# Projecting the third and fourth batch earlier in layer 0's attention

## Chip, cores and metric

One NeuronCore of a Trainium2 chip runs the whole kernel in one launch. The metric is the device time of that launch in microseconds (us), lower is better.

## What is computed

Two transformer layers on x of shape 4 x 512 x 256 (batch, sequence, width), each with attention and a mixture of experts, both modulated. Only layer 0's attention (16 heads of 16) is touched by the change:

```python
h = _layernorm(x) * (1 + ca) + sa
q, k, v = (h @ w.T + b for w, b in (wq, bq), (wk, bk), (wv, bv))   # 4 x 16 heads x 512 x 16
q, k = _apply_rope(q, k, S)
attn = softmax(einsum('bhqd,bhkd->bhqk', q, k) / sqrt(16))
ctx = einsum('bhqk,bhkd->bhqd', attn, v)
x = x + ga * (ctx @ wo.T + bo)
```

The rest (layer 0's experts, layer 1's attention, layer 1's experts) follows in the same program and is the same in both kernels.

## The kernel before

Layer 0's attention works on 16 groups G of four heads, four groups to a batch b. A **step** s is one round of a loop written out in Python; in it each engine gets, in program order, what its function (`tensor`, `vector`, `scalar`, `gpsimd`, `sync`) lists for s. Engines run their own instructions in that order and wait for others by semaphores, so the table of steps sets the order on every engine.

Group G owns steps 8G to 8G+7 for its scores. The line L778 appears twice on TensorE in each step (two matmuls, the scores of two heads), so the n-th pair of L778 in the trace starts step n. Batch b's scores are steps 32b to 32b+31: the third batch (b = 2) starts at step 64, the fourth (b = 3) at 96. The steps of a group after its scores are fixed offsets from 8G:

- every step: VectorE takes the maximum of two score rows (L790, `vector_max`). The scores of step s+2 use the same PSUM banks and wait for it.
- 8G+8: GpSimd splits the maxima (L802 and L804, `gpsimd_ncol`). 8G+9: TensorE turns them (L815, `tensor_nT`). 8G+10: ScalarE copies the row (L824), and GpSimd issues four small DMAs (L834, `gpsimd_nmax`) that put them beside the queries.
- 8G+13 to 8G+20: TensorE computes the turned scores (L854), which wait for those DMAs at 8G+13; ScalarE takes the exponential (L869, twice a step); TensorE multiplies by the values (L883) in every second step from 8G+16. The first of these waits for VectorE's transpose of the group before.
- 8G+23: VectorE transposes the sums and takes reciprocals (L900, L905), GpSimd normalises (L910); 8G+25 to 8G+27: L925, L933, L939. The output projection of a batch (L126 to L128 with a_ctx and a_wo) has steps 32b+53 and 32b+55.

Beside this, the next batch b is prepared at offsets from step 32(b-1), read from the tables XN_AT to V_AT by `ahead(s, at)`: its normalised rows (L349), their turning (L1068) and splitting into high and low halves (L1079, L1086, L1096, the last on GpSimd as `gpsimd_rows_lo`), the projections of queries (i = 0) and keys (i = 1) (L126 to L128 with h_hi_a), and values. After the second matmul group of queries or keys, VectorE turns them (`vector_rope`: L674, L678, L680), ScalarE makes the high halves (`scalar_halves`: L689, L692), GpSimd the low halves (`gpsimd_halves`: L698, twice), and SyncE writes them to HBM (L709, `sync_to`). GpSimd later issues DMAs that read them back as stacked tiles (`gpsimd_stack(half, i)`, L748 and L753): four per call. Half 2b must be there for step 32b, half 2b+1 for step 32b+16. A single buffer `later` holds the turned queries or keys, PSUM bank 7 alone serves all projections, turns and outputs, and there is one split buffer.

SyncE also fills the expert slots in HBM with a 1290 KB transfer (L195, slots<-empty) once the scores of steps 12, 36, 60, 84 and so on are done.

Of the kernel before, what the change touches and what calls it, by code (L numbers as in the profile page):

```python
# [17 lines left out]
B, S, D = 4, 512, 256  # L18
# [469 lines left out]
def attention0(k):  # L488
# [7 lines left out]
    with ExitStack() as st:  # L496
# [49 lines left out]
        def turned(b, i):  # L546

            return later if b else first_two[:, i]
# [234 lines left out]
        def vector_max(G, r):  # L783
            p, qt = divmod(r, TT)
            u = 8 * G + r
            n = 2 * (u % 2)
            if r == 0 and G >= 2:
                dve.wait_ge(*ncol_ready[G - 2])
            dve.wait_ge(*s_done[u])
            dve.tensor_reduce(nmax[:, G % 2, qt, 2 * p:2 * p + 2], psum[:, n:n + 2, :], AX.X, ALU.max,  # L790
                              negate=True).then_inc(s_max.sem, 1)
            max_done[u] = s_max.up()
# [103 lines left out]
        def vector_sums(G):  # L896
            if G:
                dve.wait_ge(*ctx_done[G - 1])
            dve.wait_ge(*pv_done[TT * G + TT - 1])
            dve.transpose(cT, psum[:, 6, :]).then_inc(s_cT.sem, 1)  # L900
            cT_done[G] = s_cT.up()
            dve.wait_ge(*cT_done[G])
            if G:
                dve.wait_ge(*ctxn_done[G - 1])
            dve.reciprocal(rinv[:, :, :], blocks[:, :, HD0:HD0 + 1]).then_inc(s_rinv.sem, 1)  # L905
            rinv_done[G] = s_rinv.up()
# [7 lines left out]
        def vector_normalise(G):  # L914
            s = k.sem("dve_ctx_norm")
            dve.wait_ge(*rinv_done[G])
            dve.tensor_tensor(blocks[:, :, 0:HD0], blocks[:, :, 0:HD0],
                              rinv[:, :, :].broadcast_to([P, TT * 4, HD0]), ALU.mult).then_inc(s.sem, 1)
            ctxn_done[G] = s.up()
# [169 lines left out]
        def vector_rows_lo(b, half):  # L1089
            norm.vector_lo(b, slice(half * 2 * P, (half + 1) * 2 * P), hi_done[b, half])  # L1090
            lo_of_split[b] = norm.split_ready[b]
# [14 lines left out]
        PER_BATCH = 8 * H0 // GROUP0  # L1106
# [5 lines left out]
        g_first, g = g, late  # L1112


        XN_AT, ROWS_AT, QK_AT, V_AT = (-3, -2, 1, 2), (-1, 3), (7, 11, 15, 19), (13, 27)

        SOONER = 8
        STATS_AT, SD_AT = 30, 8 * NG + EXP_AT  # L1120

        def ahead(s, at):

            for b in range(1, B):
                d = s - PER_BATCH * (b - 1) + (SOONER if b == 1 else 0)
                if d in at:
                    yield b, at.index(d)

        def groups(s, at, n=1, every=1):

            for G in range(NG):
                r, rest = divmod(s - 8 * G - at, every)
                if 0 <= r < n and rest == 0:
                    yield G, r
# [32 lines left out]
        def vector(s):  # L1167
            for G, r in groups(s, 0, 8):
                vector_max(G, r)
            for b, n in ahead(s, XN_AT):  # L1170
                norm.vector_xn(b, n, b * TT + n)
            for b, half in ahead(s, tuple(d + 2 for d in ROWS_AT)):
                if b == 1:
                    vector_rows_lo(b, half)
            for b, i in ahead(s, (QK_AT[1] + 1, QK_AT[3] + 1)):
                vector_rope(b, i)
            for G, r in groups(s, CTX_AT):
                vector_sums(G)
                if G == NG - 1:
                    vector_normalise(G)  # L1180
            for G, r in groups(s, CTX_AT + 2):
                vector_ctx(G)
            for G, r in groups(s, CTX_AT + 4):
                if G == NG - 1:
                    vector_ctx_lo(G)
            for b in range(B):
                d = s - PER_BATCH * b - 1
                if b < B - 1 and d in OUT_AT:
                    vector_out(b, OUT_AT.index(d))
                if b < B - 1 and d in BACK_AT:  # L1190
                    vector_back(b, BACK_AT.index(d))
                for m in range(KT):
                    if b == B - 1 and d == LAST_OUT[-1][m]:
                        vector_out(b, m)
                    if b == B - 1 and d == LAST_BACK_AT:
                        vector_back(b, m)

            d = s - PER_BATCH * (B - 1) - STATS_AT
            if 0 <= d < (B - 1) * TT:
                norm.vector_stat(d, d)  # L1200
            if d == (B - 1) * TT:
                norm.vector_mean_var(range(d))
                norm.at = slice(0, d)
            if s == SD_AT + 1:
                norm.vector_rstd()

        def scalar(s):
            for G, r in groups(s, EXP_AT, 8):
                scalar_exp(G, r, 0)
                scalar_exp(G, r, 1)  # L1210
            for G, r in groups(s, NT_AT + 1):
                scalar_nrow(G)
            for G, r in groups(s, CTX_AT + 3):
                scalar_ctx(G)
            if s == SD_AT:
                norm.scalar_sd()
            for b, half in ahead(s, ROWS_AT):
                scalar_rows(b, half)
            for b, half in ahead(s, tuple(d + 1 for d in ROWS_AT)):
                scalar_rows_hi(b, half)  # L1220
            for b, i in ahead(s, (QK_AT[0] + 1, QK_AT[2] + 1)):
                scalar_rope(b, i)
            for b, i in ahead(s, (QK_AT[1] + 2, QK_AT[3] + 2)):
                scalar_halves(b, i)
            for b, half in ahead(s, tuple(d + 1 for d in V_AT)):
                scalar_v(b, half)

        def gpsimd(s):
            for b, half in ahead(s, tuple(d + 2 for d in ROWS_AT)):
                if b > 1:  # L1230
                    gpsimd_rows_lo(b, half)
            for b, i in ahead(s, (QK_AT[1] + 3, QK_AT[3] + 3)):
                gpsimd_halves(b, i)
            for G, r in groups(s, NCOL_AT):
                gpsimd_ncol(G)
            for G, r in groups(s, NT_AT + 1):
                gpsimd_nmax(G)
            for G, r in groups(s, CTX_AT):
                if G < NG - 1:
                    gpsimd_normalise(G)  # L1240
            for G, r in groups(s, CTX_AT + 4):
                if G < NG - 1:
                    gpsimd_ctx(G)
            for b, i in ahead(s, (19, 26)):
                gpsimd_stack(2 * b, i)
            for b, i in ahead(s - SOONER if s < PER_BATCH else s, (29, 30)):
                gpsimd_stack(2 * b + 1, i)

        def sync(s):
            for b, i in ahead(s, (QK_AT[1] + 4, QK_AT[3] + 4)):  # L1250
                sync_to(b, i)
            j, rest = divmod(s - 12, 24)
            if rest == 0 and 0 <= j < len(k.fills) and k.fills[j][0] == 0:
                fill_slots(k, j, s_done[s])

        for s in range(XN_AT[0] - SOONER, PER_BATCH * B + 31):
            tensor(s)
            vector(s)
            scalar(s)
            gpsimd(s)  # L1260
            sync(s)
# [1872 lines left out]
```

## Time and profile before

| | us |
|---|---|
| median of 3 runs | 1456.45 |
| lowest and highest of them | 1448.93, 1463.96 |
| the profiled execution | 1450.06 |
| its span, first to last instruction | 1448.8 |
| layer 0's attention, steps 0 to 127 (first and last L778) | 48.9 to 306.5 |

Engine names: PE is TensorE, PEld its weight loads, DVE VectorE, ACT ScalarE, POOL GpSimd, SP SyncE. In a row of the timeline stand start, duration, engine, line, output and input, the number of instructions merged, and in brackets the idle time before and what ended it. PEclk is the clock granted to TensorE as a share of full speed. The three runs differ by 15 us, so a difference of a few microseconds can't be told from none without many pairs of runs.

### The profile page before, as it was taken

The numbers are of one execution on the slowest core, as the hardware profiler recorded it, in microseconds if no ns is written. First come the engines' busy times: TensorE is split into PE (matmuls) and PEld (weight loads), VectorE is DVE, ScalarE is ACT, GpSimd is POOL, SyncE is SP. The second block draws the span as 40 slices with busy tenths as digits, with TensorE's granted clock in tenths as the row PEclk, the third lists the DMA queues.
The fourth block names the chain that finished last, engine by engine and source line by source line (L and its number), as shares of the span: only waits on it lengthen the run. The fifth ranks groups of instructions, "written<-read, shape, count | busy, mean of one in ns | idle before, by whom it ended". The sixth has DMA issues, their size and how long they took to land.

```text
span 1448.8 us, 22556 instructions
## 1 busy us (share of the span) xinstructions
PE 1294.8 (89%) x6461; PEld 913.3 (63%) x6461; DVE 874.5 (60%) x2649; ACT 780.0 (54%) x1907; POOL 441.0 (30%) x577
## 2 busy tenths in 40 slices
PE   6689799887889998799999999999999986999994
PEld 5334344334556776577777777787777764678773
DVE  5678687753553365765577566666676754543555
ACT  3267575653431545566666556665566643166562
POOL 5344545220344644200000006001410140455553
PEclk9689898987989999899999999999999997999997
DMA  6653617003213553144200001000100018555664
GB/s 219 135 123 84 154 31 151 2 2 149 107 49 99 162 163 100 36 143 140 69 1 1 16 1 60 1 16 1 45 16 16 1 44 326 186 158 156 209 192 139
DMA packets 79207, 133.99 MB, mean 92 GB/s; under 512 B 13788, under 2 KB 52708, under 8 KB 77420
## 3 DMA queue, kind: packets, MB, share of 16 engines
q1 hardware_dynamic: 62128, 92.39, 20.8%
q0 software_dynamic: 15712, 38.25, 9.4%
q10 hardware_dynamic: 1248, 1.90, 0.4%
q8 instruction: 57, 0.93, 0.3%
q14 instruction: 62, 0.51, 0.1%
HBM read 77.20 MB, written 60.00 MB: 95 GB/s over the span
## 4 chain that ended last, share of the span: by engine, by line
PE 69%; DVE 11%; issue 6%; DMA 6%; ACT 4%; POOL 4%; DVEq 0%; SPq 0%; ACTq 0%; POOLq 0%
PE psum L126 9%; PE psum L1984 8%; PE psum L128 8%; PE psum L127 8%; PE psum L2628 7%; PE psum L2674 4%; PE psum L1955 4%; PE psum L2501 4%; PE psum L854 3%; PE psum L883 3%; PE psum L2535 2%; PE psum L2597 1%; PE psum L778 1%; DVE a_nmax L790 1%; POOL slots L1635 1%
## 5 line engine op out<-in xcount | busy, mean ns | idle before, releaser
L790 DVE TENSOR_REDUCE a_nmax<-psum 128x2 f32<-128x1024 f32 x128 | 155.1, 1217 | 66.5 <-PE psum L778 65.5
L869 ACT ACTIVATE a_et<-psum 128x512 f32<-128x512 f32 x256 | 139.0, 594 | 92.0 <-PE psum L854 88.5
L1930 ACT ACTIVATE a_spare<-psum,a_nmax 128x128 f32<-128x128 f32 (+3 forms) x256 | 134.7, 526 | 93.4 <-DVE a_nmax L1919 87.6
L1919 DVE CUSTOM_DVE_ANT_0 psum<-psum,a_spare 128x128 f32<-128x128 f32 (+3 forms) x256 | 126.7, 495 | 79.4 <-PE psum L128 78.6
L2697 POOL DMA_INDIRECT results<-r_fin,r_to x134 | 134.3, 1002 | 123.0 <-ACT r_fin L2689 63.1
L1984 PE MATMUL psum<-a_et,a_v 128*128 128x512 f32 (+3 forms) x512 | 169.5, 433 | 0.0
L2628 PE MATMUL psum<-m_w,m_xT 128*128 x536 | 150.5, 403 | 0.0
L1964 ACT ACTIVATE a_et<-psum 128x128 f32<-128x128 f32 (+3 forms) x256 | 111.6, 436 | 64.2 <-PE psum L1955 60.7
L126 PE MATMUL psum<-a_kT,a_q 128*128 128x128 f32 (+3 forms) x256 | 118.9, 465 | 6.8 <-DVE a_q L1858 5.9
L854 PE MATMUL psum<-a_stk 50*128 50x512 f32 x256 | 109.0, 500 | 15.0 <-ACT a_et L869 12.1
L1955 PE MATMUL psum<-ident,a_spare 128*128 128x128 f32 x640 | 113.5, 275 | 0.6 <-DVE a_spare L1943 0.6
L2674 PE MATMUL psum<-m_w,m_hidT 128*128 (+1 forms) x346 | 103.1, 398 | 8.4 <-DVE m_hidT L2664 7.5
L1943 DVE TENSOR_SCALAR a_spare<-a_spare,a_rinv 128x128 f32<-128x128 f32 (+3 forms) x256 | 103.7, 405 | 9.0
L1984 PEld LDWEIGHTS psum<-a_et,a_v 128*128 128x128 f32 x512 | 95.6, 189 | 18.9
L1941 DVE RECIPROCAL a_rinv<-a_rsum 128x1 f32<-128x1 f32 x256 | 41.6, 163 | 107.7 <-ACT a_spare L1930 100.5
L854 PEld LDWEIGHTS psum<-a_stk 50*128 50x128 f32 x256 | 44.1, 201 | 98.2 <-ACT a_et L869 75.4
L778 PE MATMUL psum<-a_stk 48*128 48x512 f32 x256 | 96.5, 493 | 8.6 <-DMA a_stk<-stacks 6.7
L2645 DVE TENSOR_TENSOR m_hid<-m_silu,psum 128x128 f32<-128x128 f32 (+1 forms) x134 | 40.3, 300 | 103.8 <-ACT m_silu L2638 101.8
L2628 PEld LDWEIGHTS psum<-m_w,m_xT 128*128 128x128 f32 x536 | 91.4, 190 | 13.3
L2689 ACT ACTIVATE r_fin<-psum,r_to 128x256 f32<-128x256 f32 x134 | 63.2, 472 | 45.2 <-PE psum L2674 35.4
L128 PE MATMUL psum<-a_kT,a_q 128*128 128x128 f32 (+3 forms) x256 | 83.7, 327 | 0.0
L1955 PEld LDWEIGHTS psum<-ident,a_spare 128*128 128x128 f32 x640 | 76.7, 141 | 10.9 <-issue 2.4
(326 smaller groups left out, 2940.6 us busy)
## 6 DMA issues: line engine op xcount, KB each, us to landing
r_xs<-slots SPq DMA_DIRECT2D x134, 129.0 KB, 2.3
slots<-empty SPq DMA_DIRECT2D x12, 1290.0 KB, 6.6
m_w<-in_experts SPq DMA_DIRECT2D x16, 768.0 KB, 14.3
stacks<-a_qk SPq DMA_DIRECT2D x32, 256.0 KB, 3.8
a_stk<-stacks POOLq DMA_DIRECT2D x32, 256.0 KB, 7.0
r_shared_hid<-results SPq DMA_DIRECT2D x12, 512.0 KB, 4.6
m_w<-in_experts SPq DMA_DIRECT2D x4, 1216.0 KB, 14.2
a_stk<-stacks POOLq DMA_DIRECT2D x32, 128.0 KB, 6.3
```

The source lines that it names most:

```text
L126: self.pe.matmul(out, lh, rh, start=start, stop=False, skip_group_check=True)
L128: return self.pe.matmul(out, ll, rh, start=False, stop=stop, skip_group_check=True)
L790: dve.tensor_reduce(nmax[:, G % 2, qt, 2 * p:2 * p + 2], psum[:, n:n + 2, :], AX.X, ALU.max, negate=True).then_inc(s_max.sem, 1)
L854: pe.matmul(psum[:, 4 + hh, :], pair[rows, 1, kt * P:(kt + 1) * P], pair[rows, 0, :], start=True, stop=True).then_inc(s_sT.sem, 1)
L869: act.activation(et[:, n % NET, 2 * p + hh, :], psum[:, 4 + hh, :], ACT.Exp).then_inc(s_e.sem, 1)
L1919: dve.tensor_tensor_reduce(psum[:, n, 0:W], psum[:, n, 0:W], mask[:, S - W:S], 1.0, BIG, ALU.add, ALU.min, nmax[:, u % NE, :]).then_inc(s_ ...
L1930: act.activation(e[:, u % NE, 0:W], psum[:, n, 0:W], ACT.Exp, bias=nmax[:, u % NE, :], scale=-1.0, accum_out=rsum[:, u % NE, :]).then_inc( ...
L1955: mm = pe.transpose(psum[:, n, c:c + P], e[:, u % NE, kt * P:(kt + 1) * P], k.ident[:, :])
L1984: mm = pe.matmul(psum[:, n, kt * P:S], v[:, b % 2, kt, h // HPG1 * HD1:(h // HPG1 + 1) * HD1], queries(i, kt), start=(kt == 0), stop=(kt = ...
L2628: mm = pe.matmul(psum[:, n, 0:2 * hid], xT[:, i % NT3, j, :], w[:, bass.ds(start_of[i] + j * 2 * hid, 2 * hid)], start=(j == 0), stop=(j = ...
L2674: mm = pe.matmul(psum[:, n, 0:D], hdT[:, i % NT2, c, :], w[0:CH, bass.ds(start_of[i] + KT * 2 * hid + c * D, D)], start=(c == 0), stop=(c ...
L2697: pool.indirect_dma_start(results[:, :], bass.IndirectOffsetOnAxis(ap=to[:, i % NI, 0:1].bitcast(U32), axis=0), ys[:, o, :], None, bounds_ ...
```

## The change

For b = 2 and 3 the tables get other numbers; b = 1 keeps its steps. Offsets are from step 32(b-1).

| for b = 2, 3 | before | after |
|---|---|---|
| normalised rows XN_AT | -3, -2, 1, 2 | -7, -6, -3, -2 |
| turned and split ROWS_AT | -1, 3 | -5, -1 |
| queries, keys QK_AT | 7, 11, 15, 19 | 3, 7, 11, 13 |
| values V_AT | 13, 27 | 15, 19 |
| stacks of half 2b | 19, 26 | 15, 20 |
| stacks of half 2b+1 | 29, 30 | 29, 30 |

```diff
-        XN_AT, ROWS_AT, QK_AT, V_AT = (-3, -2, 1, 2), (-1, 3), (7, 11, 15, 19), (13, 27)
-        SOONER = 8
+        XN_AT = [None, (-11, -10, -7, -6)] + [(-7, -6, -3, -2)] * (B - 2)
+        ROWS_AT = [None, (-9, -5)] + [(-5, -1)] * (B - 2)
+        QK_AT = [None, (-1, 3, 7, 11)] + [(3, 7, 11, 13)] * (B - 2)
+        V_AT = [None, (5, 19)] + [(15, 19)] * (B - 2)
+        STACK_AT = [None, (11, 18, 29, 30)] + [(15, 20, 29, 30)] * (B - 2)
...
-            for b, i in ahead(s, (19, 26)):
-                gpsimd_stack(2 * b, i)
-            for b, i in ahead(s - SOONER if s < PER_BATCH else s, (29, 30)):
-                gpsimd_stack(2 * b + 1, i)
+            for b, j in ahead(s, STACK_AT):
+                gpsimd_stack(2 * b + j // 2, j % 2)
```

The followers keep their distances: the rope of i one step after its second projection (offsets 8 and 14 now, 12 and 20 before), the high halves two, the low halves three (10 and 16 now, 14 and 22 before), the write four. No instruction is added or taken away.

On GpSimd, while the fourth batch is prepared (steps 78 to 90), the order before is this: low halves of the queries, then normalise and ncol of one group, nmax, and the first stacks of half 6 after them.

```order
L698 TENSOR_TENSOR a_qk<-a_turned,a_qk 128x512 x2
L910 TENSOR_TENSOR a_turn_work<-a_turn_work,a_rinv 128x16x16
L802 CAST a_ncol<-a_nmax 128x4x4
L804 TENSOR_TENSOR a_ncol<-a_nmax,a_ncol 128x4x4
L834 DMA a_stk<-a_nrow 2x512 x4
L939 TENSOR_TENSOR a_ctx<-a_turn_work,a_ctx 128x512
L753 DMA a_stk<-stacks 32x2048 x2
L753 DMA a_stk<-stacks 16x2048 x2
L698 TENSOR_TENSOR a_qk<-a_turned,a_qk 128x512 x2
```

The same engine at the same group (normalise at step 79, ncol at step 80) after the change:

```order
L910 TENSOR_TENSOR a_turn_work<-a_turn_work,a_rinv 128x16x16
L753 DMA a_stk<-stacks 32x2048 x2
L753 DMA a_stk<-stacks 16x2048 x2
L698 TENSOR_TENSOR a_qk<-a_turned,a_qk 128x512 x2
L802 CAST a_ncol<-a_nmax 128x4x4
L804 TENSOR_TENSOR a_ncol<-a_nmax,a_ncol 128x4x4
L834 DMA a_stk<-a_nrow 2x512 x4
L939 TENSOR_TENSOR a_ctx<-a_turn_work,a_ctx 128x512
```

Four stack DMAs and the two low halves of the keys have come to stand between the normalising and ncol. The same stands at steps 47 and 48, for the third batch.

On VectorE the rope of the queries (L674 to L680) stood between the maxima of steps 76 and 77, three maxima ahead of the next transpose:

```order
L674 SCALAR_TENSOR_TENSOR a_turned<-psum,a_bias,a_rope 128x512
L678 TENSOR_TENSOR a_turned<-a_turned,a_rope 128x512
L680 TENSOR_TENSOR a_turned<-a_turned 128x512
L790 TENSOR_REDUCE a_nmax<-psum 128x2 x3
L900 STREAM_TRANSPOSE a_turn_work<-psum 128x512
L905 RECIPROCAL a_rinv<-a_turn_work 128x16
```

After the change it is the rope of the keys, between the maxima of steps 78 and 79, one maximum ahead of the same transpose:

```order
L674 SCALAR_TENSOR_TENSOR a_turned<-psum,a_bias,a_rope 128x512
L678 TENSOR_TENSOR a_turned<-a_turned,a_rope 128x512
L680 TENSOR_TENSOR a_turned<-a_turned 128x512
L790 TENSOR_REDUCE a_nmax<-psum 128x2
L900 STREAM_TRANSPOSE a_turn_work<-psum 128x512
L905 RECIPROCAL a_rinv<-a_turn_work 128x16
```

The rope moved two maxima nearer to the transpose of step 79.

## Rows read from the trace of the kernel before

**Rows 1.** The page, the chain that ended last, by engine.
```profile
PE 69%; DVE 11%; issue 6%; DMA 6%; ACT 4%; POOL 4%; DVEq 0%; SPq 0%; ACTq 0%; POOLq 0%
```

**Rows 2.** Timeline, ends of the second and third batch: stack issues, slot fill, first scores after.
```profile
163.90 2.00 POOL L753 DMA_DIRECT2D a_stk<-stacks  x4
164.16 0.38 SPq L195 DMA_DIRECT2D slots<-empty  x1
176.88 0.80 PE L778 MATMUL psum<-a_stk 48*128 48x512 f32 x2 [6.28 <-DMA a_stk<-stacks]
...
242.39 0.50 PE L778 MATMUL psum<-a_stk 48*128 48x512 f32 x2 [0.43 <-DMA a_stk<-stacks]
```

**Rows 3.** DMA issues landing in 160 to 180: KB each, median us to landing.
```profile
a_stk<-stacks POOLq DMA_DIRECT2D x6, 256.0 KB, 9.9
...
a_stk<-a_nrow POOLq DMA_DIRECT2D x4, 4.0 KB, 1.6
```

**Rows 4.** Windows: length, busy times of PE, PEld, DVE, ACT, POOL, PEclk, DMA share, GB/s.
```profile
171.40:185.00 13.60, 8.12 (x31) 2.87 (x31) 5.04 (x7) 4.66 (x9) 2.49 (x5) 0.50 0.74 167
185.00:243.10 58.10, 55.70 (x336) 26.95 (x336) 46.62 (x51) 40.29 (x76) 30.39 (x50) 1.00 0.39 95
243.10:256.70 13.60, 13.29 (x53) 4.97 (x52) 7.33 (x8) 6.99 (x13) 4.36 (x8) 0.50 0.56 80
338.60:359.10 20.50, 14.88 (x50) 11.50 (x51) 9.50 (x40) 6.53 (x15) 0.46 (x4) 0.50 0.52 198
```

**Rows 5.** Timeline, PE: scores of steps 67, 102, 104, 107 and 110.
```profile
185.11 0.72 PE L778 MATMUL psum<-a_stk 48*128 48x512 f32 x2
...
256.86 0.72 PE L778 MATMUL psum<-a_stk 48*128 48x512 f32 x2
...
259.88 0.63 PE L778 MATMUL psum<-a_stk 48*128 48x512 f32 x2
...
265.41 0.72 PE L778 MATMUL psum<-a_stk 48*128 48x512 f32 x2
...
270.38 0.72 PE L778 MATMUL psum<-a_stk 48*128 48x512 f32 x2
```

**Rows 6.** Timeline, POOL, steps 78 to 84.
```profile
205.00 2.53 POOL L698 TENSOR_TENSOR a_qk<-a_turned,a_qk 128x512 fp32r<-128x512 f32 x2 [2.33 <-ACT a_qk L689]
210.04 0.62 POOL L910 TENSOR_TENSOR a_turn_work<-a_turn_work,a_rinv 128x256 f32<-128x256 f32 x1 [2.52 <-DVE a_rinv L905]
...
210.89 0.22 POOL L804 TENSOR_TENSOR a_ncol<-a_nmax,a_ncol 128x16 fp32r<-128x16 f32 x1
...
218.07 2.01 POOL L753 DMA_DIRECT2D a_stk<-stacks  x4
```

**Rows 7.** Timeline, PE and DVE, steps 77 to 81.
```profile
202.96 0.74 DVE L674 SCALAR_TENSOR_TENSOR a_turned<-psum,a_bias,a_rope 128x512 f32<-128x512 f32 x1
...
204.34 0.69 DVE L680 TENSOR_TENSOR a_turned<-a_turned 128x512 f32<-128x512 f32 x1
...
205.38 0.72 PE L778 MATMUL psum<-a_stk 48*128 48x512 f32 x2
...
208.97 0.70 DVE L900 STREAM_TRANSPOSE a_turn_work<-psum 128x512 f32<-128x512 f32 x1
...
210.11 1.07 PE L883 MATMUL psum<-a_et,a_v 128*32 128x512 f32 x8
210.27 1.22 DVE L790 TENSOR_REDUCE a_nmax<-psum 128x2 f32<-128x1024 f32 x1 [0.31 <-PE psum L778]
...
211.78 0.66 PE L815 MATMUL psum<-a_ident_r,a_ncol 128*128 128x128 f32 x4
```

**Rows 8.** Timeline, steps 72 to 77: scores of 72, the nmax DMAs, scores of 77.
```profile
193.98 0.72 PE L778 MATMUL psum<-a_stk 48*128 48x512 f32 x2
...
199.26 2.10 POOL L834 DMA_DIRECT2D a_stk<-a_nrow  x4 [3.57 <-ACT a_nrow L824]
...
202.73 0.72 PE L778 MATMUL psum<-a_stk 48*128 48x512 f32 x2
```

**Rows 9.** Timeline, PE: a wait after the attention's steps.
```profile
340.18 0.80 PE L126 MATMUL psum<-a_ctx,a_wo_hi 128*128 128x512 f32 x1 [3.69 <-DVE a_ctx L945]
```

More of the change, by code:

```diff
@@ L1112, in attention0, with ahead @@
         g_first, g = g, late
-        XN_AT, ROWS_AT, QK_AT, V_AT = (-3, -2, 1, 2), (-1, 3), (7, 11, 15, 19), (13, 27)
-        SOONER = 8
+        XN_AT = [None, (-11, -10, -7, -6)] + [(-7, -6, -3, -2)] * (B - 2)
[3 more added lines that the diff above has]
+        STACK_AT = [None, (11, 18, 29, 30)] + [(15, 20, 29, 30)] * (B - 2)
         STATS_AT, SD_AT = 30, 8 * NG + EXP_AT
-        def ahead(s, at):
+        def ahead(s, at, every=1, after=0):
             for b in range(1, B):
-                d = s - PER_BATCH * (b - 1) + (SOONER if b == 1 else 0)
-                if d in at:
-                    yield b, at.index(d)
+                d, steps = s - PER_BATCH * (b - 1) - after, at[b][every - 1::every]
+                if d in steps:
+                    yield b, steps.index(d)
         def groups(s, at, n=1, every=1):
@@ L1171, in vector @@
                 norm.vector_xn(b, n, b * TT + n)
-            for b, half in ahead(s, tuple(d + 2 for d in ROWS_AT)):
+            for b, half in ahead(s, ROWS_AT, after=2):
                 if b == 1:
                     vector_rows_lo(b, half)
-            for b, i in ahead(s, (QK_AT[1] + 1, QK_AT[3] + 1)):
+            for b, i in ahead(s, QK_AT, 2, 1):
                 vector_rope(b, i)
@@ L1218, in scalar @@
                 scalar_rows(b, half)
-            for b, half in ahead(s, tuple(d + 1 for d in ROWS_AT)):
+            for b, half in ahead(s, ROWS_AT, after=1):
                 scalar_rows_hi(b, half)
-            for b, i in ahead(s, (QK_AT[0] + 1, QK_AT[2] + 1)):
-                scalar_rope(b, i)
-            for b, i in ahead(s, (QK_AT[1] + 2, QK_AT[3] + 2)):
+            for b, j in ahead(s, QK_AT, after=1):
+                if j % 2 == 0:
+                    scalar_rope(b, j // 2)
+            for b, i in ahead(s, QK_AT, 2, 2):
                 scalar_halves(b, i)
-            for b, half in ahead(s, tuple(d + 1 for d in V_AT)):
+            for b, half in ahead(s, V_AT, after=1):
                 scalar_v(b, half)
         def gpsimd(s):
-            for b, half in ahead(s, tuple(d + 2 for d in ROWS_AT)):
+            for b, half in ahead(s, ROWS_AT, after=2):
                 if b > 1:
                     gpsimd_rows_lo(b, half)
-            for b, i in ahead(s, (QK_AT[1] + 3, QK_AT[3] + 3)):
+            for b, i in ahead(s, QK_AT, 2, 3):
                 gpsimd_halves(b, i)
@@ L1243, in gpsimd @@
                     gpsimd_ctx(G)
-            for b, i in ahead(s, (19, 26)):
-                gpsimd_stack(2 * b, i)
-            for b, i in ahead(s - SOONER if s < PER_BATCH else s, (29, 30)):
-                gpsimd_stack(2 * b + 1, i)
+            for b, j in ahead(s, STACK_AT):
+                gpsimd_stack(2 * b + j // 2, j % 2)
         def sync(s):
-            for b, i in ahead(s, (QK_AT[1] + 4, QK_AT[3] + 4)):
+            for b, i in ahead(s, QK_AT, 2, 4):
                 sync_to(b, i)
@@ L1254, in sync @@
                 fill_slots(k, j, s_done[s])
-        for s in range(XN_AT[0] - SOONER, PER_BATCH * B + 31):
+        for s in range(XN_AT[1][0], PER_BATCH * B + 31):
             tensor(s)
```

## Prediction

> **What bounds the kernel now.** I read the chain of waits first: TensorE carries 69% of it, so what counts is when TensorE waits and at which clock it runs [rows 1]. The change is confined to layer 0's attention, so I read the timeline there step by step. Two places belong to the stacks. At the third batch's first scores (step 64) TensorE waits 6.28 us for the stack DMAs; at the fourth's (step 96) 0.43 us [rows 2]. The reader is to see why the first is so long: the last four stack DMAs were issued from 163.90 on, and 0.26 us later SyncE started the 1290 KB slot fill, so they landed only at 176.9. The DMAs of that kind took 9.9 us to land in this stretch [rows 3]. The windows then show what a wait costs besides itself: TensorE's granted clock was at the lower level (0.50, 1.2 GHz) from 171.4 to 185.0 and from 243.1 to 256.7, and at the upper level (1.00, 2.4 GHz) between them [rows 4]. In other steps TensorE is nearly saturated while projections are in (55.7 of 58.1 us busy from 185.0 to 243.1).
>
> **What the change removes.**
> The stack load of half 4 that was late is issued at step 52 instead of 58, ahead of the fill at step 60. Step 64 then finds its data: -6.3 us. For the fourth batch the second load moves from step 90 to step 84, about where the first stood before (218.07) [rows 6]. That is 24 us ahead of step 96, against 9.9 to land even with a fill beside it. That saves 0.4 us, and up to 0.9 with what stands behind it; I take -0.9.
> With the wait the slow clock behind it goes. Its price is read by comparing equal steps: 64 to 66 took 185.11 - 176.88 = 8.2 us at the lower clock, 104 to 106, with the same scores and values, 265.41 - 259.88 = 5.5 [rows 2, 5]. That is -2.7. The fall at 243.1 costs 256.86 - 242.39 = 14.5 us for steps 96 to 101 against 270.38 - 259.88 = 10.5 for 104 to 109: 4.0 us. It came just as the fourth batch began with little in it but scores and a stack wait. Without that wait it may stay away or come elsewhere, as the stretch before step 96 now has less filling. I take it as gone (-4.0), and keep 0 as the other end.
> Sum of gains: 6.3 + 0.9 + 2.7 + 4.0 = 13.9 us; 9.9 if the second fall stays.
>
> A rule weighed: the Trainium skill, "DMA: Bandwidth & Descriptors", section on the anatomy of one DMA by the GpSimd path, fits a DMA's time as 2.0 us plus bytes over 436 thousand per us. By it a 256 KB stack load would land in an estimated 2.6 us, the loads of 163.90 would be in before step 64, and the change would remove nothing. This trace disagrees (9.9 us, and a wait of 6.28), because the fill shares the engines; the measurement decides.
>
> **What the moves put in the way.** All counts of instructions stay, so the price is in waits. I work it in the fourth batch's preparation (steps 72 to 81); the third's (40 to 49) repeats it.
>
> *The keys' rope, one maximum ahead of the transpose.* Rope takes 204.34 + 0.69 - 202.96 = 2.07 us [rows 7]. It comes after the maximum of step 78, which starts about 0.77 behind the scores of that step (205.38) and takes 1.22: done 207.4, rope 209.4, maximum of 79 at 210.7, L900 at 211.3. TensorE's value matmul (L883) of step 80 started at 210.11 and must wait for L900: now 211.35. Cost 1.2 us. What hid the rope before was the values' projection in the same step and two more maxima of slack.
>
> *GpSimd's queue.* Normalising (L910) started 0.37 us after L900 had ended (208.97 + 0.70) and takes some 0.6: now it is done at 212.2. Before, ncol followed at once: L804 ended at 211.11, and TensorE's L815 ran at 211.78, so there were 0.67 us of slack [rows 6, 7]. Now four stack issues (2.01 us) and two low halves (2.53) stand ahead of ncol [rows 6]: 212.2 + 2.0 + 2.5 + 0.5 = 217.3. GpSimd's queue is in order, and TensorE's too: behind L815 wait the scores and everything else. TensorE is at L815 0.67 + 1.0 us after L883, at 213.0, and waits until 217.3: 4.3 us. So the two together set it back by 217.3 - 211.8 = 5.5 us. The bounds: if normalising began as early as before (210.04), ncol would be ready at 215.6, 3.9 us late, which is the low end; nothing in GpSimd's order can make it less unless L753 doesn't hold the engine, and rows 6 show it does. The high end is 6.5, with a late high half.
>
> *The queries' rope and halves, at steps 72 to 74.* Rope stands after the maximum of step 72, with no projection beside it but that of step 75. Maximum done 196.0, rope 198.1, maximum of 73 at 199.3; the scores of step 75, which stood at about 198.8, wait 0.5 us. GpSimd's halves end about 200.6 where nmax was issued at 199.26 [rows 8]; its fourth DMA is issued 1.6 later and takes 1.6 to land [rows 3]: 203.8, against step 77 at 202.73 + 0.5. Another 0.5. Together 1.0 us, between 0 and 2.
>
> *The splitting of rows* (GpSimd 1.3 us, at step 29 now) comes just ahead of eight stack issues (4 us) and the ncol of step 32. Before, it stood behind that ncol. I take 0.5 us, between 0 and 1.3.
>
> Other moves have one answer: the same projections use bank 7 in steps of their own as before (every odd step is taken once in both), the values are ready by step 20 of a batch that needs them at 48, and the write of the keys has 4 steps before its load. Cost 0; the cover is that no two users of bank 7 meet.
>
> Sum of waits per batch: 5.5 + 1.0 + 0.5 = 7.0 us, twice is 14.0.
>
> *The clock behind the new wait.* TensorE was granted the lower level from 0.8 us after it had begun to wait at step 64. A wait of 3.69 us that ended at 340.18 also lay at the edge of a stretch at 0.50, from 338.6 to 359.1 [rows 4, 9]. The wait of 4.3 us at step 81 lies between the two in length. I take it that the clock falls again for 13.6 us, some 2 to 3 of which lie in the wait itself. Of slow time, 4.0 of 14.5 us is lost, 28%, and more where projections saturate TensorE (up to half). For 11 us: 3 to 5.5; I take 4.1. Bounds 0 (no fall) and 6.8. Twice is 8.2.
>
> **The sum.** -13.9 + 14.0 + 8.2 = +8.3 us against the profiled execution's 1450.06 (span 1448.8): 1458.4. The median of the runs shown is 1456.45, 6.4 higher than the profiled one, so on that base it is 1464.8. I predict 1464; the change pays for the wait that it removes with two new ones.
>
> **Rivals.**
> *The gain comes whole.* The new waits would have to be absorbed, if GpSimd got through sooner than its rows add up to, or if TensorE's place in step 81 were late anyway. For it speaks only that L815 was never the bound before; against it the order on GpSimd and durations from rows. With 1 to 4 us left of the waits: -13.9 + 3, so 1445 on the median's base. Chance 0.17.
> *Slower by more.* Both ncol waits bring the clock down in the heaviest steps (two output projections stand in steps 85 and 87), and the fall at 243 stays, or comes in the now emptier steps 88 to 96. Then -9.9 + 14.0 + 2 x 6 = +16, 1472; it decides as soon as a fall in the attention is added to two at L815. With the high ends, +20. Chance 0.26.
> *Waits without falls.* The stalls at L815 are there, but TensorE keeps the upper clock: -13.9 + 14.0, so no change, 1456.5. For it: the fall at 243.1 came with hardly any wait, so wait and fall aren't tied one to one; against it, the two long waits in the rows both had one. Chance 0.15.
> *The change doesn't do what it says*: the load of half 4 waits for its write or its free slot and is late again. Its write follows 4 steps before as it did, and the slot was free by step 45. Then 0 + 14.0 + 8: +22, 1478. Chance 0.02.
> My forecast, both stalls and both falls and the old fall gone: 0.40.
>
> **The numbers.** The forecast's own range is 1459 to 1470. The runs of one kernel differ by 15 us, so I widen by some microseconds on each side: 1448 to 1477 leaves out most of the whole gain and the tail of the slower one. Changes under 1%, 14.6 us, can't be told well from none. Faster by over 1% needs the whole gain and more: 0.08. Slower by over 1%: most of the second rival and the edge of the forecast, 0.27. Within: 0.65.
>
> **What would show it.** In the profile after: no wait of L778 for stacks (right about the gain); L815 waiting some 4 us for POOL L804 twice, near 142 and 205 (the main step); L883 waiting for L900 by 1.2 us just before; PEclk 0.50 in windows behind both; at 172 and 235 the upper level. If L815 doesn't wait, or by less than 2 us, the step on GpSimd's queue is wrong and the time is near 1445. If it waits but PEclk stays at 1.00, it is near 1456.

## The result, and the profile after

| | before | after |
|---|---|---|
| median of 4 runs, us | 1456.97 | 1476.70 |
| lowest and highest | 1448.93, 1463.96 | 1473.68, 1481.98 |
| ratio of the runs, 95% interval | | 1.0144 [1.011, 1.0177] |
| profiled execution, us | 1450.06 | 1473.68 |
| its span | 1448.8 | 1472.4 |

The change makes the kernel slower by 1.4%, some 20 us. I forecast 1464, slower by 8.

The chain of the kernel after, by engine; it answers to [rows 1]:

```profile
PE 68%; DVE 11%; issue 8%; POOL 4%; DMA 4%; ACT 4%; another core or an unknown queue 1%; SPq 0%; DVEq 0%; ACTq 0%; POOLq 0%
```

It says little: TensorE leads as before. Where the time went is read by the starts of the same step (the first L778 of a step) in the two traces:

| step starts, us | before | after | block before it: before | after | difference |
|---|---|---|---|---|---|
| 0 | 48.89 | 47.34 | | | |
| 32 | 107.32 | 107.46 | 58.4 | 60.1 | +1.7 |
| 64 | 176.88 | 188.24 | 69.6 | 80.8 | +11.2 |
| 96 | 242.39 | 263.88 | 65.5 | 75.6 | +10.1 |
| 127 | 304.54 | 322.21 | 62.2 | 58.3 | -3.8 |

Steps 0 to 127 take 19.2 us more. The blocks that lose are the two in which the third and the fourth batch are prepared, and the first of them loses 11.2 us although its wait of 6.28 us for the stacks [rows 2] is gone. (The two spans differ by 23.6: the attention began 1.5 us sooner after the change, and the code behind it, which is the same, took 5.9 us longer in that execution.)

The longest waits of TensorE in the attention of the kernel after (48 to 345 us), by the line that waited and the work it waited for: total us, times, longest:

```profile
PE psum L854 <- DMA a_stk<-a_nrow: 13.2, 9, 3.4
PE psum L854 <- ACT a_et L869: 11.6, 19, 1.8
PE psum L815 <- POOL a_ncol L804: 8.5, 2, 4.3
PE psum L883 <- DVE a_turn_work L900: 4.6, 9, 0.7
PE psum L778 <- DVE a_nmax L790: 2.5, 4, 1.0
```

Against the same view of the kernel before, L854 waits 11.0 us more for the small nmax DMAs (2.2 before, no single one over 0.6), L815 8.3 more for ncol (0.2 before), L883 2.1 more and L778 0.8 more for the maxima; the waits of L778 for stacks (6.7, two of them) are gone. The sum is +15.5 of the 19.2 us. The largest entry is not the one that I forecast.

The timeline of the kernel after around the third batch's preparation. First the wait for ncol, then those for nmax (start, duration, engine, line; in brackets the idle time before, and what ended it):

```profile
144.46 1.07 PE L883 MATMUL psum<-a_et,a_v 128*32 128x512 f32 x8 [0.65 <-DVE a_turn_work L900]
...
144.77 0.62 POOL L910 TENSOR_TENSOR a_turn_work<-a_turn_work,a_rinv 128x256 f32<-128x256 f32 x1 [12.65 <-DVE a_rinv L905]
145.33 2.03 POOL L753 DMA_DIRECT2D a_stk<-stacks  x4
...
147.38 2.49 POOL L698 TENSOR_TENSOR a_qk<-a_turned,a_qk 128x512 fp32r<-128x512 f32 x2
...
150.08 0.22 POOL L804 TENSOR_TENSOR a_ncol<-a_nmax,a_ncol 128x16 fp32r<-128x16 f32 x1
...
150.44 1.09 PE L815 MATMUL psum<-a_ident_r,a_ncol 128*128 128x128 f32 x4 [4.25 <-POOL a_ncol L804]
...
230.30 1.09 PE L815 MATMUL psum<-a_ident_r,a_ncol 128*128 128x128 f32 x4 [4.26 <-POOL a_ncol L804]
```

These are the engines and lines of [rows 6, 7] in their new order: normalising, 2.03 us of stack issues, 2.49 us of low halves, and only then ncol. TensorE waits 4.25 and 4.26 us, where 4.3 was forecast.

```profile
128.72 2.09 POOL L834 DMA_DIRECT2D a_stk<-a_nrow  x4
128.76 2.81 SPq L709 DMA_DIRECT2D stacks<-a_qk  x4
134.16 0.76 PE L854 MATMUL psum<-a_stk 50*128 50x512 f32 x1 [2.36 <-DMA a_stk<-a_nrow]
...
174.90 2.12 POOL L834 DMA_DIRECT2D a_stk<-a_nrow  x4 [5.66 <-ACT a_nrow L824]
...
176.58 0.38 SPq L195 DMA_DIRECT2D slots<-empty  x1
...
181.05 0.58 PE L854 MATMUL psum<-a_stk 50*128 50x512 f32 x1 [3.42 <-DMA a_stk<-a_nrow]
```

Two things are to be seen. SyncE's write of the queries' halves (L709) now starts in the same microsecond as the nmax DMAs (L834), 0.04 us apart; the fourth batch repeats it (209.37 beside 209.31, a wait of 2.40). And the slot fill, which before started beside the stack loads at 164.16 [rows 2], now starts while the nmax DMAs of 174.90 are being issued. In the first case the landing is told by the view of DMA issues of 120 to 135:

```profile
stacks<-a_qk SPq DMA_DIRECT2D x4, 256.0 KB, 3.8
a_stk<-a_nrow POOLq DMA_DIRECT2D x4, 4.0 KB, 3.3
```

An nmax DMA of 4 KB lands after 3.3 us (the median of the four), against 1.6 in [rows 3].

TensorE's granted clock by windows (length, busy times, then PEclk, DMA share, GB/s), which answer to [rows 4]:

```profile
133.50:140.30 6.80, 6.13 (x22) 3.06 (x22) 2.08 (x2) 2.17 (x4) 0.00 (x0) 0.50 0.06 22
147.10:157.40 10.30, 6.96 (x28) 3.90 (x29) 3.43 (x4) 3.18 (x7) 6.37 (x10) 0.50 0.74 170
181.30:188.10 6.80, 6.80 (x28) 2.73 (x26) 4.40 (x6) 3.26 (x6) 2.45 (x6) 0.50 1.06 196
215.40:218.80 3.40, 3.40 (x10) 2.33 (x10) 1.22 (x1) 1.03 (x2) 0.00 (x0) 0.50 0.00 0
229.00:239.30 10.30, 9.00 (x36) 5.28 (x36) 2.45 (x2) 3.26 (x7) 6.38 (x12) 0.50 0.60 142
239.30:331.40 92.10, 79.00 (x463) 34.10 (x462) 68.68 (x77) 58.07 (x110) 28.36 (x56) 1.00 0.19 37
```

Each of the five waits has a stretch at 0.50 (1.2 GHz) that begins in it or just behind it; a wait of 1.75 us at 103.0 has none. The fall that came at 243.1 before is not in this trace: 1.00 (2.4 GHz) holds from 239.3 to 331.4.

### The profile page after: what moved, and what is told of

It is laid out like the page before. It is cut to its first block, busy times and chain, and to the rows that moved or that the text cites. A ratio compares the mean times of both kernels' runs of the same rounds, so it can differ in the third digit from the quotient of the medians.

```text
span 1472.4 us, 22556 instructions
## 1 busy us (share of the span) xinstructions
PE 1299.2 (88%) x6461; PEld 914.9 (62%) x6461; DVE 872.5 (59%) x2649; ACT 779.4 (53%) x1907; POOL 441.7 (30%) x577
## 4 chain that ended last, share of the span: by engine, by line
PE 68%; DVE 11%; issue 8%; POOL 4%; DMA 4%; ACT 4%; another core or an unknown queue 1%; SPq 0%; DVEq 0%; ACTq 0%; POOLq 0%
PE psum L126 9%; PE psum L1983 8%; PE psum L128 8%; PE psum L127 8%; PE psum L2627 7%; PE psum L2673 5%; PE psum L1954 4%; PE psum L2500 3%; PE psum L854 3%; PE psum L883 2%; PE psum L2534 2%; PE psum L2596 2%; PE psum L778 1%; DVE psum L1918 1%; POOL slots L1634 1%
## 5 line engine op out<-in xcount | busy, mean ns | idle before, releaser
L854 PE MATMUL psum<-a_stk 50*128 50x512 f32 x256 | 108.5, 492 | 26.2 <-DMA a_stk<-a_nrow 13.2
L126 PE MATMUL psum<-a_kT,a_q 128*128 128x128 f32 (+3 forms) x256 | 118.9, 464 | 6.9 <-DVE a_q L1857 5.9
L854 PEld LDWEIGHTS psum<-a_stk 50*128 50x128 f32 x256 | 43.7, 198 | 108.1 <-ACT a_et L869 74.8
L778 PE MATMUL psum<-a_stk 48*128 48x512 f32 x256 | 96.6, 489 | 2.5 <-DVE a_nmax L790 2.5
L2673 PEld LDWEIGHTS psum<-m_w,m_hidT 128*128 128x128 f32 (+1 forms) x346 | 56.7, 188 | 43.7 <-issue 36.3
```

The source lines that it names most:

```text
L126: self.pe.matmul(out, lh, rh, start=start, stop=False, skip_group_check=True)
L854: pe.matmul(psum[:, 4 + hh, :], pair[rows, 1, kt * P:(kt + 1) * P], pair[rows, 0, :], start=True, stop=True).then_inc(s_sT.sem, 1)
L2673: mm = pe.matmul(psum[:, n, 0:D], hdT[:, i % NT2, c, :], w[0:CH, bass.ds(start_of[i] + KT * 2 * hid + c * D, D)], start=(c == 0), stop=(c ...
```

## The experiments

Two theories stood at the outset. By the first, the wait of L815 behind GpSimd's new order, with the clock fall behind it, is most of the loss. By its rival, the nmax DMAs meet larger transfers (the moved write, the fill), and that costs as much. Ratios below are to the kernel before on the same chip, with 95% intervals; the first four share one chip (before: median 1446.32), the next four another (1454.69), the last a third (1447.80).

**ncol ahead of the halves and stacks** (edits of the changed kernel).

```diff
-        STACK_AT = [None, (11, 18, 29, 30)] + [(15, 20, 29, 30)] * (B - 2)
+        STACK_AT = [None, (11, 18, 29, 30)] + [(17, 20, 29, 30)] * (B - 2)
...
-            for b, i in ahead(s, QK_AT, 2, 3):
-                gpsimd_halves(b, i)
             for G, r in groups(s, NCOL_AT):
                 gpsimd_ncol(G)
+            for b, i in ahead(s, QK_AT, 2, 3):
+                gpsimd_halves(b, i)
```

> The changed kernel with GpSimd's order put back around ncol: the first stacks of half 2b at offset 17 instead of 15, and the low halves behind ncol in their step, for the third and fourth batch. Theory 1 (GpSimd's queue holds ncol back): the two waits of L815 for POOL L804 (4.25 us each) shrink below 0.7 us, and what the clock lost behind them (some 2 to 4 us each) comes back, so 12 to 16 us less than the changed kernel, 1461 to 1465. The waits of L854 for the nmax DMAs near 132 and 212 stay, since nothing moves there. Rival (the engines were late at that point anyway, L815 is only where it shows): the waits move to L883 or L854 two steps on and the time stays within 4 us of the changed kernel's.

Measured: 1478.32 us, 1.0200 [1.0163, 1.0237], no gain over the change where 12 to 16 us were expected. The wait of L815 for GpSimd is gone, so what made it is right. But its place was taken, four steps on, by L854 at steps 53 and 85. Timeline and waits of this kernel:

```profile
148.62 2.04 POOL L753 DMA_DIRECT2D a_stk<-stacks  x4
148.70 3.07 SPq L709 DMA_DIRECT2D stacks<-a_qk  x4
...
150.64 2.05 POOL L834 DMA_DIRECT2D a_stk<-a_nrow  x4
...
160.14 0.77 PE L854 MATMUL psum<-a_stk 50*128 50x512 f32 x1 [7.12 <-DMA a_stk<-a_nrow]
...
248.38 0.76 PE L854 MATMUL psum<-a_stk 50*128 50x512 f32 x1 [7.93 <-DMA a_stk<-a_nrow]
```
```profile
PE psum L854 <- DMA a_stk<-a_nrow: 28.1, 9, 7.9
```

The four small DMAs are issued right behind four stack loads and beside a write of four, and land 5.8 to 7.8 us after issue; TensorE waits 7.12 us. At 248.38 it waits 7.93, and there the slot fill was issued among them too, at 239.48. Together these two are 15 us where the removed waits were 8.5. Whether the engines were late at L815 anyway, the rival, can't be told from this kernel; the one with GpSimd's order mended, below, decides it.

**The queries' write two steps later.**

```diff
-        STACK_AT = [None, (11, 18, 29, 30)] + [(15, 20, 29, 30)] * (B - 2)
+        STACK_AT = [None, (11, 18, 29, 30)] + [(17, 20, 29, 30)] * (B - 2)
...
             for b, i in ahead(s, QK_AT, 2, 4):
-                sync_to(b, i)
+                if b == 1 or i == 1:
+                    sync_to(b, i)
+            for b, i in ahead(s, QK_AT, 2, 6):
+                if b > 1 and i == 0:
+                    sync_to(b, i)
```

> The changed kernel with SyncE's write of the third and fourth batch's queries two steps later (six steps behind the second projection instead of four), and the first stacks that read them two steps later (17), behind ncol. Theory 2 (the four 256 KB writes share the DMA engines with the 4 KB nmax DMAs that are issued in the same microsecond, so these land after 3.3 us instead of 1.6): the waits of L854 for nmax near 132 and 212, 2.4 us each, fall below 0.9 us, nmax lands in 1.6 us again. Rival A (the nmax DMAs are late because GpSimd issues them behind the low halves): the waits stay above 1.5 us. As a by-product theory 1 says that without the four stack issues ahead of ncol the wait of L815 is 2.2 us instead of 4.25, the two low halves alone being left.

Measured: 1467.37 us, 1.0114 [1.0072, 1.0156], an interval that overlaps with the change's. On the write it decides nothing, because the edit didn't move it: SyncE issued it at 134.97, nmax was issued from 134.91, and the waits of 2.70 and 2.44 us stayed. SyncE has hardly anything else to do in these steps, so it runs to its next instruction, and only what that instruction waits for sets its time. What the edit does show is the part of the stacks in the other wait:

```profile
154.97 0.64 PE L815 MATMUL psum<-a_ident_r,a_ncol 128*128 128x128 f32 x4 [2.24 <-POOL a_ncol L804]
```

With the four stack issues (2.0 us) moved behind ncol, 4.25 became 2.24; the low halves are the rest. The moved stacks, with the keys' write beside them, met the next nmax (a wait of 3.43 us at 166.16).

**The fill two steps later, in the changed kernel**; and **the same edit in the kernel before**.

```diff
-            j, rest = divmod(s - 12, 24)
+            j, rest = divmod(s - 14, 24)
```

> The changed kernel with SyncE's slot fills two steps later (steps 14, 38, 62, 86 instead of 12, 36, 60, 84). Theory 3 (the 1290 KB fill of step 60 started while the last nmax DMA of the group was under way, and that is the 3.4 us wait of L854 at 177.6 and the slow clock from 181.3): that wait falls below 1 us and the slow clock behind it goes, 4 to 6 us less than the changed kernel. Rival (the wait comes from GpSimd, whose rows_lo and stacks stand there now): the wait stays above 2 us. The two waits of L815 stay at 4.2 in both.

> The kernel before with nothing changed but the slot fills two steps later (62 instead of 60 for the one that matters). If the 6.28 us wait at step 64 comes from the fill sharing the DMA engines with the stack loads of 163.90, the loads land in 3 to 6 us and the wait is below 1 us: 6 to 9 us less than before with the clock's part, 1447 to 1451. Rival (eight more stack issues behind the four are what delays them, since they land behind each other): the wait stays above 3 us, and the time within 4 us of before.

Measured, in the changed kernel: 1469.37 us, 1.0152 [1.0114, 1.019]; 4 to 6 us less than the change were expected, and no gain shows. The wait at step 61 fell from 3.42 to 0.59 us, so the fill had made it. But the fill now starts at 181.20, beside eight stack loads issued from 180.77, and the next nmax waits 3.16 us at 196.65.

Measured, in the kernel before: 1441.92 us, 0.9962 [0.9935, 0.9989]. The stack wait of step 64 (6.28 us) is gone altogether; the one that is left, 0.47 us, is that of step 96. A part came back in the same way; its timeline:

```profile
161.87 2.01 POOL L753 DMA_DIRECT2D a_stk<-stacks  x4
...
165.12 0.38 SPq L195 DMA_DIRECT2D slots<-empty  x1
...
173.88 2.10 POOL L834 DMA_DIRECT2D a_stk<-a_nrow  x4 [1.74 <-ACT a_nrow L824]
...
180.36 0.76 PE L854 MATMUL psum<-a_stk 50*128 50x512 f32 x1 [3.60 <-DMA a_stk<-a_nrow]
...
236.55 0.50 PE L778 MATMUL psum<-a_stk 48*128 48x512 f32 x2 [0.47 <-DMA a_stk<-stacks]
```

So 6.28 us for stacks became 3.60 for nmax, and the kernel is 0.4% faster. That is the whole aim of the change, reached by one number of the fill.

**The write waits until nmax has landed.** Since a step number doesn't hold SyncE back, a wait must.

```diff
             for b, i in ahead(s, QK_AT, 2, 4):
+                if b > 1 and i == 0:
+                    sp.wait_ge(*nmax_in[(s - 10) // 8])
                 sync_to(b, i)
```

> The changed kernel in which SyncE holds the write of the third and fourth batch's queries back until the nmax DMAs of that group have landed; nothing else. It repeats, with a wait that really holds, what the later step in e2_write_later did not do (SyncE issued the write in the same microsecond as before, since a step alone does not delay an engine that waits for nothing else). Theory 2 (the four writes share the DMA engines with nmax): nmax lands in 1.6 us there, and L854's two waits of 2.4 us before step 45 and 77 fall to 0.3 to 0.9. Rival A (GpSimd issues nmax too late, behind the low halves): they stay above 1.5 us. Time in the first case 3 to 7 us less than the changed kernel's, which stood at 1.0144 of before: 1.010 to 1.012. The L815 waits of 4.25 stay.

Measured: 1468.12 us, 1.0072 [1.0043, 1.0101], a little below the 1.010 to 1.012 expected. The timeline:

```profile
127.89 2.09 POOL L834 DMA_DIRECT2D a_stk<-a_nrow  x4
...
131.06 2.62 SPq L709 DMA_DIRECT2D stacks<-a_qk  x4
131.18 0.47 PE L854 MATMUL psum<-a_stk 50*128 50x512 f32 x1 [0.21 <-DMA a_stk<-a_nrow]
...
145.23 1.08 PE L815 MATMUL psum<-a_ident_r,a_ncol 128*128 128x128 f32 x4 [4.27 <-POOL a_ncol L804]
```

The write starts 3.17 us after the first nmax issue instead of 0.04, and TensorE's wait falls from 2.36 to 0.21 us. GpSimd's issues are the same in both, so it was the transfers beside the small ones that delayed them, and not a late issue. L815 and the fill keep their waits (4.27, 4.26; 4.23 at 176.2). Steps 40 to 46 and 72 to 78 took 13.7 us each, 4.8 and 3.7 less than in the changed kernel. Steps 0 to 127 as a whole took 275.1 us all the same, against 274.9: this execution (1474.94 us, above its kernel's median) had TensorE at 0.50 from 175.0 to 195.5, in and behind the fill's wait, and again from 257.0 to 274.0. So that the two waits go is shown by the trace, and that the kernel gets faster by the runs alone.

**And GpSimd's order mended.** To the kernel above: the keys' low halves three steps later and their write two, behind the nmax DMAs and L939, and the first stacks behind both.

```diff
-        STACK_AT = [None, (11, 18, 29, 30)] + [(15, 20, 29, 30)] * (B - 2)
+        STACK_AT = [None, (11, 18, 29, 30)] + [(19, 22, 29, 30)] * (B - 2)
...
             for b, i in ahead(s, QK_AT, 2, 3):
-                gpsimd_halves(b, i)
+                if b == 1 or i == 0:
+                    gpsimd_halves(b, i)
...
+            for b, i in ahead(s, QK_AT, 2, 6):
+                if b > 1 and i == 1:
+                    gpsimd_halves(b, i)
...
-                sync_to(b, i)
+                if b == 1 or i == 0:
+                    sync_to(b, i)
+            for b, i in ahead(s, QK_AT, 2, 6):
+                if b > 1 and i == 1:
+                    sync_to(b, i)
```

> The projections stay where the change put them. GpSimd's share is placed around nmax: the keys' low halves at offset 19 behind the context instead of 16, the stacks of half 2b at 19 and 22, and the queries' write waits for nmax as in e5_write_waits. Theories 1 and 2 together: no wait of L815 for POOL L804, no wait of L854 for nmax above 1 us between steps 40 and 58 and 72 and 90. Left are the wait of 3.4 us at step 60 behind the slot fill and the one of 1.75 us at step 28. The time is then 1.0144 minus some 20 us, 1.000 of before, within 0.004. If GpSimd's and the DMA engines' order is not what cost the time, it stays above 1.008.

Measured: 1456.57 us, 1.0006 [0.998, 1.0033]. L815 no longer waits for GpSimd, and no nmax wait of 7 us took its place, as one had in the first experiment. So the engines had not been late there anyway: 1468.12 became 1456.57 on the same chip. The edit moves three things at once, so it doesn't tell what each is worth. The waits for nmax, of which the one that the fill makes is the largest (3.76 us at 170.03):

```profile
PE psum L854 <- DMA a_stk<-a_nrow: 9.6, 10, 3.8
```

**And the fill behind an nmax.** To the kernel above:

```diff
-            j, rest = divmod(s - 12, 24)
+            j, rest = divmod(s - 13, 24)
             if rest == 0 and 0 <= j < len(k.fills) and k.fills[j][0] == 0:
-                fill_slots(k, j, s_done[s])
+                fill_slots(k, j, nmax_in[(s - 11) // 8])
```

> e6_order, and the slot fills wait for the landing of the nmax DMAs of the group (fill of step 61 behind nmax of step 58) instead of the scores of step 60. Theory 3 in its second form (a large transfer must start when the nmax DMAs have just landed; two steps later, in e3_fill_later, it only met the next ones): no wait of L854 for nmax above 1 us after step 40 except by chance, no wait of L778 for stacks, and the time below before by 5 to 10 us, a ratio of 0.993 to 0.997. Rival: the eight stack loads of step 61 and 62 and the fill together still reach the nmax of step 66, with a wait over 2 us before step 69.

Measured: 1450.62 us, 0.9969 [0.994, 0.9997]. Its waits and one window of the clock:

```profile
PE psum L854 <- DMA a_stk<-a_nrow: 6.7, 11, 1.6
```
```profile
106.70:297.80 191.10, 171.03 (x1022) 78.48 (x1024) 150.17 (x164) 128.94 (x244) 81.96 (x139) 1.00 0.35 81
```

No wait of that kind is over 1.6 us (behind step 40 the longest is 1.43, at step 93, where at most 1 was expected), none is for stacks, and TensorE has the upper clock through 191 us, past both preparations. Steps 32 to 95 take 129.2 us (135.1 before, 156.4 after the change).

**And the keys' rope back by two steps**, away from the transpose. To the kernel above:

```diff
-        QK_AT = [None, (-1, 3, 7, 11)] + [(3, 7, 11, 13)] * (B - 2)
-        V_AT = [None, (5, 19)] + [(15, 19)] * (B - 2)
+        QK_AT = [None, (-1, 3, 7, 11)] + [(3, 7, 11, 15)] * (B - 2)
+        V_AT = [None, (5, 19)] + [(13, 19)] * (B - 2)
...
-            for b, i in ahead(s, QK_AT, 2, 6):
+            for b, i in ahead(s, QK_AT, 2, 4):
...
-            for b, i in ahead(s, QK_AT, 2, 6):
+            for b, i in ahead(s, QK_AT, 2, 4):
```

> e7_order_fill with the values at offsets 13 and 19 and the last projection of the keys at 15 instead of 13, so that the keys' rope on VectorE comes behind the transpose of the sums (offset 16) and not ahead of it (14). If the rope ahead of the transpose costs what was worked out (1.2 us each, of which the traces show 0.7 as L883 waiting for L900 and the rest in the maxima), the ratio is 0.001 to 0.002 below e7's. Rival: it is no more than a shift of 1 us that comes back at step 19, and the two agree within 1 us.

Measured: 1448.80 us, 0.9968 [0.9937, 0.9998], the same as without it. The waits of L883 for the transpose fell, from the first row (the kernel above) to the second (this one):

```profile
PE psum L883 <- DVE a_turn_work L900: 4.8, 9, 0.7
```
```profile
PE psum L883 <- DVE a_turn_work L900: 2.6, 6, 0.6
```

but steps 40 to 55 took 35.9 us against 35.6: what L883 waits less, others wait more. The rope's place costs nothing that shows.

**The kernel before, with only the fill of step 60 moved**, to step 69 and behind an nmax.

```diff
-            j, rest = divmod(s - 12, 24)
-            if rest == 0 and 0 <= j < len(k.fills) and k.fills[j][0] == 0:
-                fill_slots(k, j, s_done[s])
+            j, rest = divmod(s - 12 - (9 if s == 69 else 0), 24)
+            if s != 60 and rest == 0 and 0 <= j < len(k.fills) and k.fills[j][0] == 0:
+                fill_slots(k, j, nmax_in[7] if s == 69 else s_done[s])
```

> The kernel before with one slot fill moved: the one of step 60 goes out at step 69, when the nmax DMAs of step 66 have landed. e4_before_fill_later took away the stack wait of step 64 (0.5 us left of 6.28) but its fill met the nmax DMAs of step 66 (a wait of 3.6 us). If a 1290 KB transfer costs nothing when it starts just behind nmax, neither the stack wait nor a wait above 1 us at step 69 is seen, and the ratio to before is 0.992 to 0.996, below e4's 0.996. That would say that the whole gain that the change was to bring is had without moving a projection. Rival: the clock falls at other places instead, and the ratio is 0.997 or above although both waits are gone.

Measured: 1444.47 us, 0.9960 [0.9924, 0.9996]. The nmax wait of 3.60 us that the kernel with all fills moved had at step 69 is down to 1.40, not below the 1 us that was expected. The fill was issued only at 183.22, behind the four landings, so of the large transfers only the stack loads were still under way beside them:

```profile
183.34 0.47 PE L854 MATMUL psum<-a_stk 50*128 50x512 f32 x1 [1.40 <-DMA a_stk<-a_nrow]
```
```profile
PE psum L854 <- DMA a_stk<-a_nrow: 3.7, 3, 1.8
```

Stacks cost 0.4 us in all, at step 96. (The profiled execution, 1457.36 us, was the longest of the twelve; only these waits are read from it.) Yet the ratio is that of the kernel with all fills moved (0.9962), within the intervals; the rest of a few us can't be told at this spread. The kernel before with one fill moved, and the change mended in three places, are equally fast: 0.3 to 0.4% under the kernel before, with intervals that end just below 1. I found no version that is faster than these.

## Why the prediction was wrong in size

The direction of the sum was right, and so were the two waits that carried it. The size was not: 1464 forecast, 1476.7 measured, at the upper edge of the range and past the 1% bound to which I gave 0.27. By terms, the sum over steps 0 to 127:

| term | forecast, us | measured, us |
|---|---|---|
| stack waits | -7.2 | -6.7 |
| L815 for ncol, two | +8.6 | +8.3 |
| L883 behind the rope | +2.4 | +2.1 |
| L854 for nmax | +2 | +11.0 |
| L778 for the maxima | +1 | +0.8 |
| clock and everything else | +1.5 | +3.7 |
| sum | +8.3 | +19.2 |

The measured waits are differences between the two views of waits; the last term is what is left of 19.2. Read step by step, the rows agree less well than the table does. The forecast is split from my text: of its 14.0 us, 8.6 for L815, 2.4 for L883, 1.0 for L778, and 2 for nmax (0.5 at step 77 and 0.5 for the splitting of rows, twice each); the clock is -2.7 - 4.0 + 8.2.

*The gain: right in the waits, not shown in the clock.* No wait for stacks is left. The fall at 243.1 stayed away too, and the last block, from step 96 on, is 3.8 us shorter, where I took 4.0. That this is the change's doing isn't shown, and it may be luck: the kernel with the rope moved back has no stack wait either, and in its profiled execution (1459.06 us, the longest of the twelve) TensorE ran at 0.50 for 41 us there, with no wait above 1.2 us at its start:

```profile
237.40:278.40 41.00, 38.95 (x148) 14.57 (x148) 23.48 (x24) 19.39 (x36) 12.29 (x24) 0.50 0.23 40
```

Its last block took 69.0 us, against 62.2 before and 58.3 after the change.

*GpSimd's queue: right* to 0.05 us per wait, and nearly so in its two parts (2.0 for the stacks; 2.24 for the halves, where I had 2.5). The clock fell at both. Steps 47 to 52 took 7.8 us more and steps 79 to 84 9.1, against 9.6 forecast for wait, rope and fall together. The waits ended at 150 and 230 instead of "near 142 and 205". The second of these places was a slip: my own sum ends that wait at 217.3.

*The rope: too high by nearly half.* Behind the rope L883 waits 0.65 and 0.72 us (steps 48 and 80) where 1.2 was forecast. That the row comes to 2.1, near my 2.4, is luck: the other 0.8 us lie at steps 64 and 96, with no rope ahead of them. And the kernel in which L883 waits 2.2 us less was no faster.

*The maxima: not there.* I had the scores of step 75, and of its like in the third batch, wait 0.5 us each. L778 waits for no maximum in either preparation; its waits lie in steps 2 to 11, in both kernels. The 0.8 beside my 1.0 is luck.

*The step that failed* is in the part on the queries' halves: "its fourth DMA is issued 1.6 later and takes 1.6 to land [rows 3]: 203.8, against step 77 at 202.73 + 0.5. Another 0.5." I counted GpSimd's issue time and gave the landing its old price. With the halves SyncE's write moved too, into the same microsecond, and the landing took 3.3 us. The wait was 2.4 us, twice (steps 45 and 77), with a stretch at the lower clock of its own behind each (133.5 to 140.3, 215.4 to 218.8). Steps 40 to 46 took 5.4 us more, steps 72 to 78 4.2, where I had 1.0 each. The kernel in which only this write waits shows it: 2.36 us became 0.21. These two are 4.8 of the 11.0 us that the row of nmax has over before; the fill's wait at step 61 is 3.4, steps 29 and 93 have 1.2 and 1.0, and step 101 about 0.5.

*"Cost 0"* failed with it. I followed the moved DMAs to their own readers ("the write of the keys has 4 steps before its load"), and never asked which small DMA stands beside them. The same with the values: without their projection at offset 27, step 59 took 1.61 us instead of 2.30, and the fill of step 60, which the diff doesn't touch, came while the nmax of 174.90 was under way; before, it had started 0.26 us after an issue of stacks, which only slowed those. That made 3.42 us at step 61 and a stretch at 0.50 (181.3 to 188.1). That the fill makes the wait is shown by moving it; that the shorter step brought the two together is only read from the two traces.

*The splitting of rows*: I had 0.5 us for it, ahead of the ncol of step 32, and no wait for ncol is there. What stands near it is an nmax wait of 1.75 us at 103.0 (step 29), 0.56 before. The splitting (L1096) can't have made it: it starts at 102.27, when all four nmax DMAs are issued. No large transfer is under way either, and still the fourth lands 2.9 us after its issue. What does start between is a small transfer of the queue that the profile calls instruction; from the view of 94 to 103:

```profile
q8 instruction: 1, 0.02, 0.7%
```

All eight kernels with the projections moved have such a transfer at step 28 and this wait (1.36 to 1.93 us). The three with the old places have it at step 30, behind the landings, and at most 0.56 us. No kernel here tests whether the one makes the other.

*The rivals.* "Slower by more" gave 1472, near to what came, but for another reason: it needed the fall at 243 to stay or come elsewhere, and both falls at L815 at a high price. What came were new falls behind waits that it didn't contain. "Waits without falls" is out, and so is "the gain comes whole". The rule on a DMA's time that I weighed (the Trainium skill, "DMA: Bandwidth & Descriptors", section on the anatomy of one DMA by the GpSimd path) fails more widely than I used it: by it a DMA of 4 KB would land in an estimated 2.0 us. Here the same one took 1.6 alone, 3.3 beside a write of 4 x 256 KB and up to 7.8 behind stack loads and a write; the measurement decides.

*How the loss divides*, by kernels that mend one part after the other: 1.0144 for the change, 1.0072 once the write waits, 1.0006 with GpSimd's order, 0.9969 with the fill. At 1456 us that is 10, 10 and 5 us (the first is between two chips and give or take some 6; the other two, run against run on one chip, give or take some 4). The part that I had costed is the second of these three, and no larger than the one that I had taken for 1 us a batch.

Two things stay open. The 5.9 us behind the attention in the profiled execution come from no work that the change touches. In the traces of all these kernels the same code behind step 127 took from 1139 to 1154 us, so a difference of the attention in one trace need not show in the runs. And the mended kernel's 0.9969 against the 0.996 of the kernel before with one fill moved says that projecting sooner gives nothing that can be measured here; that it gives exactly nothing isn't shown.

## What to carry to other kernels

Before a step is moved, list for each small DMA with a short deadline (here nmax: issued at 8G+10, needed at 8G+13) which large transfers start from its issue to its landing, before and after; price it by its landing beside such a transfer and not by its landing alone. Do that also for transfers that the diff doesn't name, since a step that gets shorter moves them as well. To keep a large transfer out of such a stretch, let it wait until the small one has landed: a later step number holds nothing back on a queue that has nothing else to do.

## What the runs showed of the hardware beyond that

A 4 KB DMA issued by GpSimd 2 us behind its own four stack loads, with SyncE's write of 4 x 256 KB under way, took 5.8 to 7.8 us to land; the view of DMA issues of the first experiment, 150.6 to 153:

```profile
stacks<-a_qk SPq DMA_DIRECT2D x1, 256.0 KB, 9.1
a_stk<-stacks POOLq DMA_DIRECT2D x1, 128.0 KB, 7.9
a_stk<-a_nrow POOLq DMA_DIRECT2D x4, 4.0 KB, 6.1
```

And the slow stretches differed in length: 6.8, 10.3, 6.8, 3.4 and 10.3 us behind waits of 2.36, 4.25, 3.42, 2.40 and 4.26 us, against 13.6 behind one of 6.28 before. I had carried 13.6 over to the waits of 4.3. The length is not told by the wait: the stretch of 41 us in the kernel with the rope moved back had no wait above 1.2 us at its start.
